# Two buffers each for the upper and lower parts of the attention's features

## The reference

```python
x = x + attn(gru(cond_2048, x))                        # GRU cell over 32 steps, then attention
x = x + ffn(oscillator(cond_2048, cond_2048, x))       # a coupled oscillator (RK4), then a quantized FFN

# attn: q, k, v = h @ W + b, split into 4 heads of 64
scores  = einsum("bdsh,bdth->bdst", q, k) / 2
weights = softmax(scores, axis=-1)
feats   = einsum("bdst,bdth->bdsh", weights, v)
return feats @ Wo + bo
```

## Time and profile before

| | us |
|---|---|
| median of 3 runs | 609.02 (607.81 to 610.57) |
| the profiled execution | 608.98 |
| its span, first to last instruction | 607.1 |

### The profile page before, as it was taken

How to read it: one execution, slowest core, us unless ns; L and a number is a source line. 1 busy time by engine, 2 the same in 40 slices (tenths; PEclk the granted TensorE clock), 3 DMA queues, 4 the chain that set the end, 5 groups by cost and what they waited for, 6 DMA issues and landing times.

```text
span 607.1 us, 17261 instructions
## 1 busy us (share of the span) xinstructions
PE 572.4 (94%) x6460; PEld 518.9 (85%) x6460; DVE 499.6 (82%) x1523; ACT 388.9 (64%) x959; POOL 250.2 (41%) x399
## 2 busy tenths in 40 slices
PE   9999999999999988988988999999999999999997
PEld 8999999999999876777776888888888888888885
DVE  3777677776776776566799999999999999999996
ACT  3554454544445453455446888888888888888785
POOL 0423233232332243420144465565565565565550
PEclk9999999999999999999899999999999999999999
DMA  8400000000000001500000000000000000000001
GB/s 263 179 3 1 1 1 2 1 1 2 1 1 1 19 4 34 146 17 3 3 0 2 10 19 10 19 18 10 19 19 11 18 19 10 18 19 11 19 19 36
DMA packets 13170, 15.08 MB, mean 25 GB/s; under 512 B 1760, under 2 KB 11296, under 8 KB 13088
## 3 DMA queue, kind: packets, MB, share of 16 engines
q1 hardware_dynamic: 13088, 13.98, 7.1%
HBM read 9.78 MB, written 4.19 MB: 23 GB/s over the span
## 4 chain that ended last, share of the span: by engine, by line
PE 75%; ACT 12%; DVE 9%; issue 3%; POOL 0%; DVEq 0%; POOLq 0%
PE PS L475 23%; PE PS L322 17%; PE PS L345 13%; ACT q_s L788 5%; PE PS L453 4%; PE PS L527 4%; PE PS L548 3%; PE PS L406 3%; PE PS L511 2%; ACT k_s L769 2%; PE PS L426 2%; PE PS L328 2%; DVE PS L1081 1%; ACT part L707 1%; ACT PS L772 1%
## 5 line engine op out<-in xcount | busy, mean ns | idle before, releaser
L475 PE MATMUL PS<-k_s,h_s 128*128 128x128 f32 x1024 | 160.7, 284 | 4.7 <-DVE PS L1055 2.5
L475 PEld LDWEIGHTS PS<-k_s,h_s 128*128 128x128 f32 x1024 | 131.7, 191 | 21.8 <-DVE PS L1069 9.8
L322 PE MATMUL PS<-part 128*128 128x256 f32 x900 | 115.6, 286 | 0.0
L322 PEld LDWEIGHTS PS<-part 128*128 128x128 f32 x900 | 109.8, 191 | 0.0
L769 ACT ACTIVATE k_s<-h_s 128x128 f32<-128x128 f32 x256 | 69.1, 305 | 50.4 <-DVE h_s L1170 29.1
L345 PE MATMUL PS<-big,wrk 128*128 128x128 f32 x744 | 88.4, 275 | 1.7 <-DVE big L926 1.7
L345 PEld LDWEIGHTS PS<-big,wrk 128*128 128x128 f32 x744 | 85.8, 192 | 2.3 <-DVE big L926 2.3
L1238 POOL COPY h_s<-big 128x256 f32<-128x256 f32 x32 | 21.5, 671 | 129.0 <-DVE big L926 129.0
L475 PE MATMUL PS<-h_s 128*128 128x128 f32 x384 | 74.2, 275 | 0.0
L475 PEld LDWEIGHTS PS<-h_s 128*128 128x128 f32 x384 | 58.3, 192 | 0.0
L664 ACT ACTIVATE big<-big 128x256 f32<-128x256 f32 x32 | 13.3, 416 | 63.2 <-DVE big L908 63.2
(11 more groups left out here) (188 smaller groups left out, 1227.8 us busy)
## 6 DMA issues: line engine op xcount, KB each, us to landing
out<-q_s SPq DMA_DIRECT2D x32, 128.0 KB, 1.7
x_s<-in_xT SPq DMA_DIRECT2D x14, 256.0 KB, 6.5
k_s<-in_wgT SPq DMA_DIRECT2D x4, 208.0 KB, 3.0
k_s<-in_wuT SPq DMA_DIRECT2D x4, 208.0 KB, 2.9
k_s<-in_wih SPq DMA_DIRECT2D x3, 256.0 KB, 4.3
wrk<-in_whh SPq DMA_DIRECT2D x3, 256.0 KB, 4.7
h_s<-in_wdT SPq DMA_DIRECT2D x3, 256.0 KB, 2.8
x_s<-in_xT SPq DMA_DIRECT2D x4, 128.0 KB, 3.9
```

The source lines that it names most:

```text
L322: r = pe.matmul(p, y, x, start=i == 0, stop=i == len(passes) - 1)
L475: return pe.matmul(PS[:, m, 0:128], w, x, start=False, stop=True, skip_group_check=True)
```

## The change

`part` grows from 9216 to 10240 columns, and `big` shrinks from 8256 to 5184, since scores, exponentials and probabilities move down to column 3072. The upper part of the features now has two buffers, at columns 6144 and 4096 of `part` (the latter held the lower parts of the q and k weights, which the attention doesn't need any more), and the lower part two at 7168 and 9216 (new). Groups use them in turn, and group 7 does too. `keep_feats(i)` of ScalarE waits from i = 2 on for both halves of `project(i-2)`. The list of free areas that the oscillator's buffers are cut from loses `big`, which it did not come to.

```diff
-        part = sb("part", [128, 9216])
+        part = sb("part", [128, 10240])
...
-        big = sb("big", [128, 8256])
+        big = sb("big", [128, 5184])
...
-        f_hi, f_lo = ([a] * 7 + [b] for a, b in ((cut(6144, 1024), v_hi[0]), (cut(7168, 1024), v_lo[0])))
+        f_hi, f_lo = ([cut(a, 1024), cut(b, 1024)] * 4 for a, b in ((6144, 4096), (7168, 9216)))
...
-        Sc, Sm, Ee, Pn = (big[:, 6144 + 512 * i:6656 + 512 * i].rearrange("p (u n) -> p u n", u=16)
+        Sc, Sm, Ee, Pn = (big[:, 3072 + 512 * i:3584 + 512 * i].rearrange("p (u n) -> p u n", u=16)
                           for i in range(4))
-        mx, sm, ri = (big[:, 8192 + 16 * i:8208 + 16 * i] for i in range(3))
+        mx, sm, ri = (big[:, 5120 + 16 * i:5136 + 16 * i] for i in range(3))
...
-        areas = [h_all[:, 2240:4096], h_all[:, 5888:8192], flat(q_s[:, :, :]), big[:, :]]
+        areas = [h_all[:, 2240:4096], h_all[:, 5888:8192], flat(q_s[:, :, :])]
...
             def keep_feats(i):
-                if 0 < i < 7:
-                    ac.wait_ge(s_o, 2 * i)
+                if i >= 2:
+                    ac.wait_ge(s_o, 2 * i - 2)
                 ac.wait_ge(s_pv, i + 1)
```

## The result

The changed kernel took 601.94 us in the median (600.31 to 604.29, 4 runs), against 608.49 us (607.81 to 610.57, 4 runs): a ratio of 0.989, 95% interval 0.985 to 0.993. Two later comparisons of the same two kernels, with more runs, gave 0.9853 (0.9828 to 0.9878) and 0.9867 (0.9831 to 0.9902). The forecast was 601.0 us, a ratio of 0.987. The profiled execution took 602.0 us, its span is 600.1 us; the profiled one before had 608.98 and 607.1.

What follows compares the result with a forecast made beforehand. TensorE was taken to be held up by ScalarE's L707, late because the only f_hi buffer was still in use. Terms 3.9 + 0.5 + 2.3 + 1.0 + 0.5 = 8.2 us gave 600.8, rounded up to 601.0 us; range 599.8 to 604.0.

Steps and rivals of the forecast that it cites:

- Values of rounds 3 to 7: TensorE, scores to values: 1.23 us instead of 2.01 from start to start, 0.78 saved five times, 3.9 us.
- The projection in round 4: TensorE, L406 to L453 in round 4: 2.02 us falls to the 1.54 of the like step, saving 0.5 us.
- The gap before project(6, 0): End of the attention: project(6, 0) could start at 286.48 instead of 288.79, held by nothing, saving 2.3 us.
- the low clock: Full clock from project(6, 0) saves 1.0 us up to feats_of(7) and 0.5 us in its first half.
- The cost of the new wait: keep_feats(7) newly waits for project(5, 1), met some 8 us before it is asked; costs nothing.
- Rounds: A round of TensorE in the attention part would take 8.83 us, against 10.09 in round 4.
- That the clock stays up I take from the same trace: Attention part: shorter pauses, 1.80 us among them, are followed by no slow matmul, so the clock should stay up.
- the two clock terms: End of the attention: 1.0 us from project(6, 0) to feats_of(7) and 0.5 us in feats_of(7), saved at full clock.
- Rival B: The clock falls all the same, near the pause before project(7, 0); last two terms lost, 602.3 us; 8%.
- Rival A: TensorE's instructions don't come fast enough: 0.34 us more per round, 1.7 over five rounds, 602.5 us; 17%.
- Rival D: GpSimd's L1262 and VectorE's L951 collide in rounds 3 to 7, 2.2 us five times, 612 us; 3%.
- Rival C: Nothing moves: another wait right behind the removed one keeps L707 late, 609 us; 3%.

Runs made afterwards that it cites:

- the old wait: The changed kernel with its moved buffers, but keep_feats(i) waits for both halves of project(i-1) again; 0.9996 of the time of the kernel before.
- the rounds alone: The changed kernel, but keep_feats(6) waits for project(5, 1) as before; 0.9925 of the time of the kernel before.
- the end alone: The changed kernel, but only keep_feats(6) and keep_feats(7) have the shorter wait; 0.9939 of the time of the kernel before.

## Why the prediction was right, and where it was not

The mechanism and the sign were right, and the time lies in the range, 0.9 us above the forecast. That it came so close is in part luck, as the balance below shows. By its steps, with the two profiled executions:

- *Values of rounds 3 to 7*, 3.9 us: 1.28, 1.21, 1.21, 1.25 and 1.22 us from scores to values instead of 2.01, together 3.9.
- *The projection in round 4*, 0.5: 0.5 (1.53 instead of 2.02).
- *The gap before project(6, 0)* and *the low clock* there, 2.3 + 1.0 + 0.5: 3.5 us up to feats_of(7) and 0.5 in its first half, 4.0 instead of 3.8.
- *The cost of the new wait* of keep_feats(7), nothing: L707 waits there for L426 alone.
- *Rounds*: 8.74, 8.90, (11.85) and 8.84 us for rounds 3 to 6 against the 8.83 worked out.

So the terms came to 8.4 us together, against 8.2, but the span became only 7.0 us shorter. Round 5 took 2.0 us more than its term allows: 0.6 by the longer pause and 1.5 by the low clock behind it. Against that, rounds 0 to 2 took 0.8 us less (21.88 instead of 22.71), for which the sum has no term. That is the luck of the execution: with the old wait the same rounds took 22.44 us in one profile and 22.13 in another, and they hold several pauses under "issue". What is left of the difference are steps of 0.1 to 0.2 us. (A small reading was off: the copy L692 of round 4 started at 247.63, not at 247.74. Nothing hangs on it.)

What fell short is the sentence "That the clock stays up I take from the same trace", because the shorter pauses there are followed by no slow matmul. That was one execution. In others the clock falls behind just those pauses: in the changed kernel in round 5 in all three profiles (about 1.5 us in the first: 1.94 + 2.62 instead of 1.53 + 1.51), in the kernel with the rounds alone in round 2. So the two clock terms, 1.5 us, agree with the mean of many runs, since there is one long pause less to fall behind, but they don't hold for a single execution. At the full clock on both sides the gain is 606.96 - 600.29 = 6.7 us, which agrees with the sum of the other three terms, 3.9 + 0.5 + 2.3; but these are few runs, and none of them was profiled. Rival B, at 8%, was thus too low and named the wrong place: the low stretch did move in the profiled execution, not to project(7, 0) but to round 5.

Rival A is half right, and by the prediction's own sign for it (pauses under "issue" in rounds 3 to 7 that sum to over 1 us) it shows. It supposed a loss in every round; rounds 3, 4 and 6 have none, and the term was rightly left out there. But I let the pause of round 5 stay at 0.63 us, and it became 1.22. In the second profile of the changed kernel it is 1.49:

```profile
261.53 0.30 PE L426 MATMUL PS<-big 32*64 32x32 f32 x2 [1.49 <-issue]
```

The table of the transfers says where the growth lies: the transfer of instructions started 0.33 us later after L435 and took 0.29 us longer. Why it did is not settled. With the end alone, where the waits of rounds 3 to 7 are still there, the pause was 1.18 us as well, and with all the old waits 0.63 to 0.92, so the removed waits are not the whole cause, and its length varies from one execution to the next. The Trainium skill (Runtime: NRT & Kernel Launch, Instruction fetch mechanics) has instructions refilled in blocks of 256; the pauses at places that move with the count of instructions agree with it. That a crossing is mostly hidden, as the Trainium skill also says there, does not hold for these bursts.

Rival D did not come about: L951 takes 0.69 us in each of rounds 3 to 7. GpSimd's L1262 and VectorE's L951 in round 4:

```profile
244.74 2.37 POOL L1262 TENSOR_TENSOR part<-h_s,part 128x1024 fp32r<-128x1024 f32 x1
...
247.70 0.69 DVE L951 TENSOR_TENSOR big<-big 128x512 f32<-128x512 f32 x1
```

L1262 ends at 247.11, 2.2 us after the scores began, as worked out; L951 comes 0.6 us later and takes its 0.69 us. Rival C is excluded by the waits: L707 moved, and the values wait for nothing.

## What to carry to other kernels

A wait on an engine with much idle time is worth a second buffer when the bounding engine waits for what is queued behind it: here ScalarE's 20.8 us of waiting cost TensorE 3.6 us directly, and the sum of what TensorE waited for told the gain, not ScalarE's idleness. Count the gain from start to start of the bounding engine's groups, and keep the terms that hang on its clock apart from the others, since a single trace doesn't tell behind which of several pauses the clock falls. Here bursts of very small matmuls were best left whole: changing between small and large tiles cost more than the pauses that it removed.

## What the hardware showed that I had not expected

TensorE paused 0.63 to 1.71 us near the end of a burst of 128 small matmuls (1.4 us long), at a place that moved by exactly the number of instructions put ahead of it, and it resumed 1.27 to 1.39 us after a transfer of 16,384 bytes on the instruction queue had ended. A change from small to large tiles and back cost 0.3 us; the Trainium skill (TensorEngine Tiling (Array Packing), Key Properties) says that changing the tiling mode drains the array, and the 0.58 us against 0.26 agree with that. And the clock's fall to half is not tied to one pause: a pause of 2.23 us before project(6, 0) was followed by one in the profile before and in that with the old wait, and by none in that of the rounds alone.
